# One short product at a time between products of 512 columns, and attention's later steps one step later

## What is computed

```python
x = x + einsum('bct,bcd->bdt', x, weights[itok])          # one 128x128 weight per batch
q, k, v = (proj(x, W) for W in (Wq, Wk, Wv))             # 1024 -> 1024, 16 heads of 64
q = q * minimum(cond, 4)
scores = where(causal, q @ k.T / 8, min)                  # 128 x 128 per head
x = x + (softmax(scores) @ v) @ Wo.T
```

## Time and profile before

| what | value |
|---|---|
| median of three runs | 1571.13 us |
| the profiled execution, span | 1569.4 us |
| TensorE busy | 1559.1 us (99%) |
| VectorE, ScalarE, GpSimd busy | 980.4, 818.9, 856.6 us |
| chain that ended last | TensorE 98%, DMA 1%, SyncE 1% |

### The profile page before, as it was taken

The page is one execution under the profiler, slowest core; times in us unless marked ns, Lnnn a source line. Parts: engine busy times, 40 slices in busy tenths (PEclk is TensorE's granted clock), DMA queues, the critical chain, the costliest instruction groups (busy, mean ns, idle before and its releaser), DMA issues.

```text
span 1569.4 us, 23424 instructions
## 1 busy us (share of the span) xinstructions
PE 1559.1 (99%) x7563; PEld 1311.9 (84%) x7563; DVE 980.4 (62%) x1748; ACT 818.9 (52%) x2221; POOL 856.6 (55%) x752
## 2 busy tenths in 40 slices
PE   9999999999999999999999999999999999999999
PEld 7888888888888888888888888888888878888887
DVE  6844454443367777777766777777777754555553
ACT  6645545543366666666666666666666522222220
POOL 1545645643255566557555566675577544555552
PEclk9999999999999999999999999999999999999999
DMA  9958888865856766667677466666675696444442
GB/s 329 334 212 275 307 285 297 301 214 215 308 182 197 206 207 199 210 188 199 186 240 238 152 172 212 186 182 201 182 195 159 222 367 238 168 161 167 163 163 85
DMA packets 192299, 341.46 MB, mean 218 GB/s; under 512 B 23986, under 2 KB 116402, under 8 KB 185010
## 3 DMA queue, kind: packets, MB, share of 16 engines
q1 hardware_dynamic: 191026, 331.59, 65.8%
q10 hardware_dynamic: 1152, 8.39, 1.4%
HBM read 184.70 MB, written 134.22 MB: 203 GB/s over the span
## 4 chain that ended last, share of the span: by engine, by line
PE 98%; DMA 1%; SPq 1%; POOL 0%; issue 0%; DVE 0%; ACT 0%; DVEq 0%
PE p_PJ L710 22%; PE p_PJ L711 22%; PE p_PJ L712 22%; PE p_SC L712 6%; PE p_SC L711 6%; PE p_SC L710 6%; PE p_PV L815 4%; PE p_LP L710 1%; PE p_PV L710 1%; PE p_PV L712 1%; PE p_PV L711 1%; PE p_LP L711 1%; PE p_LP L712 1%; PE p_PV L841 1%; PE p_LP L841 1%; DMA out<-t_xr 1%
## 5 line engine op out<-in xcount | busy, mean ns | idle before, releaser
L711 PE MATMUL p_PJ<-t_XL,t_WH 128*128 128x512 f32 x1008 | 394.1, 391 | 0.0
L710 PE MATMUL p_PJ<-t_XH,t_WH 128*128 128x512 f32 x1008 | 394.1, 391 | 0.0
L712 PE MATMUL p_PJ<-t_XH,t_WL 128*128 128x512 f32 x1008 | 392.1, 389 | 0.0
L1035 ACT ACTIVATE t_PP<-t_PP,t_st 128x128 f32<-128x128 f32 x512 | 199.5, 391 | 175.4 <-DVE t_st L1211 173.9
L1333 POOL TENSOR_TENSOR t_PP<-t_PP,t_st 128x512 f32<-128x512 f32 x128 | 133.4, 1042 | 205.7 <-DVE t_st L1215 205.7
L712 PEld LDWEIGHTS p_PJ<-t_XH,t_WL 128*128 128x128 f32 x1008 | 189.3, 188 | 40.4
L710 PEld LDWEIGHTS p_PJ<-t_XH,t_WH 128*128 128x128 f32 x1008 | 190.0, 188 | 33.8
L711 PEld LDWEIGHTS p_PJ<-t_XL,t_WH 128*128 128x128 f32 x1008 | 190.0, 188 | 32.3
L1229 DVE TENSOR_REDUCE t_AT<-p_PV 64x256 f32<-64x512 f32 x252 | 171.2, 679 | 23.7 <-ACT t_AC L1053 12.0
L1339 POOL TENSOR_TENSOR t_AT<-t_AT,t_AC 128x256 f32<-128x256 f32 x126 | 117.2, 930 | 125.5 <-DVE t_AT L1229 125.5
L1336 POOL TENSOR_TENSOR t_PS<-t_PT,t_PS 128x512 fp32r<-128x512 f32 x122 | 157.7, 1293 | 0.0
(11 more groups left out here) (254 smaller groups left out, 3545.8 us busy)
## 6 DMA issues: line engine op xcount, KB each, us to landing
t_XH<-xth_scratch SPq DMA_DIRECT2D x56, 512.0 KB, 6.5
t_XL<-xtl_scratch SPq DMA_DIRECT2D x56, 512.0 KB, 6.9
t_PT<-t_TB SPq DMA_DIRECT2D x580, 32.0 KB, 2.3
v_scratch<-t_VR SPq DMA_DIRECT2D x64, 256.0 KB, 4.5
xth_scratch<-t_XH SPq DMA_DIRECT2D x16, 1024.0 KB, 4.0
xtl_scratch<-t_XL SPq DMA_DIRECT2D x16, 1024.0 KB, 6.5
t_VX<-v_scratch SPq DMA_DIRECT2D x32, 512.0 KB, 5.7
at_scratch<-t_AT SPq DMA_DIRECT2D x126, 128.0 KB, 3.5
```

Source lines behind the costliest of these rows:

```text
L710: pe.matmul(bank, lh, rh, start=first, stop=False, skip_group_check=goes_on)
L711: pe.matmul(bank, lh, rl, start=False, stop=False, skip_group_check=goes_on)
L712: return pe.matmul(bank, ll, rh, start=False, stop=last, skip_group_check=goes_on)
L1035: act.activation(PP[:, u, h, :], PP[:, u, h, :], ACT.Exp, bias=st[:, 0, u, h:h + 1], scale=1.0, accum_out=st[:, 1, u, h:h + 1]).then_inc(a ...
```

## The change

Ticks become twelfths of a step, and each of the three matmuls of a 512-column product gets a third of a step of its own. Transposes, scores and values are put one by one a sixth of a step (`BETWEEN`) behind such a matmul: the four transposes from q + 5 1/6 on, the twelve score matmuls of a cell over four steps instead of two bursts, and the four value matmuls of a half over a step and a third. Where two kinds fall into the same gap, they stand side by side there. The anchor a moves from 21 to 22 steps, and with it all that hangs on it: scores, masks, exponentials, reciprocals, norms, turns, moves, halves, values and their sums, on all engines. `q_ev`, `kh_ev`, `kl_ev`, the splits at `quiet(cell)`, the loads and the output blocks keep their steps. The eight transposes of batch 0 stay a burst. One wait of the turn at cell 58 is joined by the usual one. The rest of the diff passes the new index m, h or k through.

```diff
-TICK = 4
+TICK = 12
+BETWEEN = 1 / 6
...
                 l0_a.put(q, (bb, h))
                 l0_x1.put(q + 0.75, (bb, h))
-                l0_b.put(q + 5, (bb, h))
+                for k in range(4):
+                    l0_b.put(q + 5 + BETWEEN + k / 3, (bb, h, k))
...
             for i in range(7):
                 for d in range(4):
-                    P_at.put(t + 4 * i + d, (p, i, d))
+                    for m in range(3):
+                        P_at.put(t + 4 * i + d + m / 3, (p, i, d, m))
...
                     for d in range(DC):
-                        step_at.put(t0 + 16 * c + 8 * i + d, (kind, n, d))
+                        for m in range(3):
+                            step_at.put(t0 + 16 * c + 8 * i + d + m / 3, (kind, n, d, m))
...
-                a = done + 5
+                a = done + 6
                 for u in range(GB):
                     k = u // 2
-                    sc_at.put(a + k, GB * n + u)
+                    for m in range(3):
+                        sc_at.put(a - 1 + u + BETWEEN + m / 3, (GB * n + u, m))
                     mask_at.put(a + 1 + 2 * k, GB * n + u)
...
-                    for z in range(2):
-                        pv_at.put(v, 2 * P + z)
+                    for i in range(4):
+                        pv_at.put(v + BETWEEN + i / 3, (2 * P + i // 2, i % 2))
...
-        def three(bank, lh, ll, rh, rl, first, last, goes_on=False):
-            pe.matmul(bank, lh, rh, start=first, stop=False, skip_group_check=goes_on)
-            pe.matmul(bank, lh, rl, start=False, stop=False, skip_group_check=goes_on)
+        def one(m, bank, lh, ll, rh, rl, first, last, goes_on=False):
+
+            if m == 0:
+                return pe.matmul(bank, lh, rh, start=first, stop=False, skip_group_check=goes_on)
+            if m == 1:
+                return pe.matmul(bank, lh, rl, start=False, stop=False, skip_group_check=goes_on)
             return pe.matmul(bank, ll, rh, start=False, stop=last, skip_group_check=goes_on)
 
+        def three(*operands):
+            one(0, *operands)
+            one(1, *operands)
+            return one(2, *operands)
...
-        def pe_values(U):
+        def pe_values(U, h):
             n, u, z = U // GB, U % GB, U % 2
             j, c = divmod(n, NC)
             P = U // 2
-            if z == 0:
+            if z == 0 and h == 0:
                 pe.wait_ge(pool_pt, P + 1)
...
-            elif n == 58:
-                dve.wait_ge(s_O, 32 * 32)
             elif k == 0:
                 dve.wait_ge(l_P, 160 * n)
+            if n == 58:
+                dve.wait_ge(s_O, 32 * 32)
```

More of the change, by code:

```diff
@@ L304, in cond_attention @@
             l0_x1.put(-4 + h, (0, h))
-            l0_b.put(-3 + h, (0, h))
+            for k in range(4):
+                l0_b.put(-3 + h, (0, h, k))
             l0_X.put(-2 + 0.75 * h, (0, h))
@@ L421, in cond_attention @@
         turns = [(b, half) for half in (1, 0) for b in range(GB)]
-        x1_load = At()
+        x1_load, out_step, out_add = At(), At(), At()
         for o in range(N_OUT):
+            for d in range(DC):
+                for m in range(3):
+                    out_step.put(T_END + 8 * o + d + m / 3, (o, d, m))
+            out_add.put(T_END + 8 * o + 7.75, o)
             x1_load.put(T_END + ((-4, -4, 8, 10)[o] if o < 4 else 8 * o - 20), o)
@@ L732, in pe_step @@
             n = 0 if kind == "q" else 1
-            if d == 0:
+            if d == 0 and m == 0:
                 pe_wait_bank(kind, item)
@@ L754, in pe_step @@
             z = x_at_(j)
-            mm = three(PJ[bank_of[kind, item]][:], lh, ll, x_chunk(XHP, z, d), x_chunk(XLP, z, d), d == 0, d == DC - 1)
-            if d == DC - 1 and kind == "q":
+            mm = one(m, PJ[bank_of[kind, item]][:], lh, ll, x_chunk(XHP, z, d), x_chunk(XLP, z, d), d == 0, d == DC - 1)
+            if d == DC - 1 and m == 2 and kind == "q":
                 mm.then_inc(pe_q, 1)
-            elif d == DC - 1:
+            elif d == DC - 1 and m == 2:
                 mm.then_inc(pe_k, 1)
@@ L812, in pe_values @@
                     pe.wait_ge(dve_M, 2 * P)
[L813 to L816, removed]
+            moving = PS[:, 2 * u + h].rearrange("p a q -> p (a q)")
+            mm = pe.matmul(PV2[:, z, 256 * h:256 * h + 256], VV[j % 2][:, u, 2 * c + h, :], moving, start=True, stop=True)
+            if h == 1:
+                mm.then_inc(pe_pv, 1)
         def pe_l0_a(bb, h):
@@ L832, in pe_l0_a, with pe_l0_b, pe_out_step @@
             three(bank[:], wh[:], wl[:], xh[h][:], xl[h][:], True, True).then_inc(pe_a, 1)
-        def pe_l0_b(bb, h):
+        def pe_l0_b(bb, h, k):
             bank = l0_bank(bb, h)
-            pe.wait_ge(act_x1, 2 * bb + h + 1)
-            if bb == 0 and h == 0:
+            if k == 0:
+                pe.wait_ge(act_x1, 2 * bb + h + 1)
+            if bb == 0 and h == 0 and k == 0:
                 pe.wait_ge(l_ident, 16)
[L839 to L847, removed]
+            tt = h * 4 + k
+            mm = pe.transpose(bank[:, k * 128:(k + 1) * 128], x_tile(bb)[:, tt * 128:(tt + 1) * 128], ident[:])
+            if k == 3:
+                mm.then_inc(pe_b, 1)
+        def pe_out_step(o, d, m):
             b, half = turns[o]
-            if d == 0:
+            if d == 0 and m == 0:
                 pe_wait_bank("o", o)
@@ L858, in pe_out_step @@
             rh, rl = wo_tile(quarter)
-            mm = three(PJ[bank_of["o", o]][:], XH[1][:, row, cols], XL[1][:, row, cols], rh[:, d % 4, :], rl[:, d % 4, :], d == 0, d == DC - 1)
-            if d == DC - 1:
+            mm = one(m, PJ[bank_of["o", o]][:], XH[1][:, row, cols], XL[1][:, row, cols], rh[:, d % 4, :], rl[:, d % 4, :], d == 0, d == DC - 1)
+            if d == DC - 1 and m == 2:
                 mm.then_inc(pe_o, 1)
@@ L1675, in sp_program @@
                     sp_load_x1(o)
-                if T_END * TICK <= tick < T_PAIR * TICK and tick % (DC * TICK) == DC * TICK - 1:
-                    o = (tick - T_END * TICK) // (DC * TICK)
+                for o in out_add(tick):
                     b, half = turns[o]
```

67 lines of the change are left out of this document (35 added, 32 removed).

## The result

The changed kernel takes 1649.3 us (median of 4 runs, 1648.71 to 1649.92) against 1571.03 us for the kernel before, measured beside it: ratio 1.0499, 95% interval 1.0484 to 1.0514. It is 78 us slower. The forecast was 42 us slower and a range that ended at 1630.

A forecast was written before the change was run, and what follows sets the result against it. TensorE's order was taken to set the time, with VectorE's own-row sum 0.73 us early. 1569.4 + 41.5 (chain) + 1.2 (transposes) - 0.3 (end of attention) = 1611.8 us; the runs' median, 1.7 over, 1613.5; range 1594 to 1630.

The forecast's parts named there:

- The chain of one cell: Attention, from one first value of half 0 to the next: 14.16 us with a split against TensorE's 13.33; 41.5 us in all.
- The split: VectorE's split of a weight piece, now ahead of half 1's own-row sum: 0.70 us in cells that have one.
- TensorE's part: First value of half 0 to end of half 1's last value: 17 large and 19 short matmuls, 6.11 us.
- the bound of +6: Attention's matmul pacing: large matmuls behind short ones dearer by 0.006 us, 0.1 a cell; zero taken, -5 to +6 kept.
- From the sum to TensorE: Handover from the end of VectorE's own-row sum to TensorE's next value: 0.05 us.
- Transposes: Pair stages: price of a transpose stays, each large matmul behind is disturbed, 62 groups x 4 x 0.005: +1.2 us.
- The end of attention: TensorE's last wait: two more large matmuls before it, -0.45 us, a queued VectorE sum about 0.2; together -0.3 us.
- a loss half as large: Rival, 8%: chain right but a link shorter than its rows, about 0.35 us a cell, 21 us: 1592.5 us.
- no change: Rival, 6%: the chain ends less than 0.73 us later and fits the margin before the value burst: 1572 us.
- faster: Rival, 6%: waits fit and short matmuls between large ones hide weight loads, 13.15 us a cell: 1560 us.
- The second wait on top: k's low part late at the first score, up to 0.2 us a cell or 12 us: 1626 us, inside the upper end.
- The upper end: Top of the forecast's own 1600 to 1628 us, made by +6 for pacing and the second wait.

The follow-up runs named there:

- shift alone: Kernel before with attention's anchor at 22 steps instead of 21, all bursts kept: 1607.58 us.
- q behind the exponentials: Changed kernel with q's high part one step later, behind the last exponential, and q's low part between the two turns: 1633.35 us.
- all splits moved: Changed kernel with q's high part behind the last exponential and the weight splits on VectorE, their stores and ScalarE's high halves 2.25 steps later: 1580.14 us.

## Why the prediction was wrong

- *What bounds the kernel, and what the margin is*: right. VectorE's own-row sum was 0.73 us early before and is the releaser now.
- *The chain of one cell*: its order was right in every link, and it closes on itself: each run that moves an item out of it shortens the cell, down to 13.35 with all of them out. Its length was 14.16 us with a split and measured 14.81; without a split 13.46 and 13.67. So the mechanism was right, and the step that failed is what three of its links cost, the split above all. Term by term, from the rows above:
  - *The split* is the step that failed most, a term that was sized too small: 0.70 was taken, 1.05 measured (714.93 to 715.98). In 48 cells 16.8 us. The row that I took the earlier trace rows was of a split that started ahead of GpSimd's next instruction. In its new place it starts behind one.
  - *TensorE's part*: 6.11 was taken, 6.30 measured (702.72 to 709.02). The first value behind a wait takes 0.19, not 0.118: 0.07 that had no term. And a large one with a short one between two large ones takes 0.35 (703.50 to 703.85), not 0.3455, some 0.12 in all: that I had kept as the bound of +6 and set to zero. In 61 cells 11.6 us.
  - *From the sum to TensorE*: 0.05 was taken, 0.15 measured (715.98 + 1.40 = 717.38 to 717.53). In 61 cells 6.1 us. The 0.05 had no row; before, nothing waited there.
  - The read, the exponentials, q's high part, reciprocal, norm and turn measured 0.81, 1.56, 0.47, 0.78 + 0.12, 0.26, 1.07 and 0.64, within 0.03 of their terms.
  - Together 34.5 us: 39.8 + 1.7 + 34.5 = 76.0, measured 74.0. The 2 us between them are in TensorE's part: it is 6.30 in the cells of 14.81 us, but 6.22 to 6.25 in those of 14.73 and of 13.67, where all later links agree within 0.04.
  - With the split alone put right the forecast would have been 1613.5 + 16.8 = 1630.3 us, at the end of the range; the other two terms are 17.7 us more.
- *Transposes*: +1.2 forecast, +1.7 measured alone (0.2 to 3.0 by the interval). The rival price (12.6 us back) is refuted.
- *The end of attention*: -0.3 forecast, +1.9 measured. The wait grew instead of shrinking by the two large ones that stand before it; I didn't test which link of it did.
- *The rivals*: a loss half as large, no change and faster are all refuted by the kernel after. (The 0.2268 of "faster" stands in no row that was shown; large matmuls in a row measure 0.2275.) The second wait on top is not in it; the run with the sum ahead of the split shows that it was near.
- *The upper end*: the two bounds that it names, 6 us for dearer matmuls and 12 for a second wait, give 1613.5 + 18 = 1631.5 us; 1628 was written. Apart from these no term of the chain could grow. It should have had the split beside GpSimd: a row of 1.24 us stood in the trace of before.

The missed price stands in the trace of before, on the other engine. GpSimd's sum of rows takes 0.73 us by itself and 1.24 when it starts behind VectorE's split at 713.51 (timeline of GpSimd in the kernel before, then in the kernel after):

```profile
713.56 1.24 POOL L1339 TENSOR_TENSOR t_AT<-t_AT,t_AC 128x256 f32<-128x256 f32 x1 [1.20 <-DVE t_AT L1229]
```
```profile
717.46 0.73 POOL L1360 TENSOR_TENSOR t_AT<-t_AT,t_AC 128x256 f32<-128x256 f32 x1 [1.95 <-DVE t_AT L1251]
```

Whichever starts second pays. The split ended some 0.55 us behind the end of GpSimd's instruction in each of four kernels: after (716.06 against 715.51), shift alone (715.75 against 715.20), q behind the exponentials (712.79 against 712.25), all splits moved (708.54 against 707.99). The Trainium skill, "SBUF — State Buffer", states under "Who interferes with whom" that a VectorE instruction with two inputs in SBUF contends with a GpSimd instruction that reads SBUF, and under "Summary: rules for kernel authors" that the second to issue blocks until the first is done. The four ends agree with it in the main: the split's length follows from where GpSimd's instruction ends (0.65 where it had ended, 1.13, 1.44), not from its own size. It is not exact: the split ends 0.55 us behind it, and its whole 0.65 after a full block would be 0.10 more. GpSimd's sum, likewise, ends 0.60 us behind the split (714.80 against 714.20), not 0.73. Which part of SBUF the two compete for, no run here shows. k's low part, with one input in PSUM, takes its 0.68 at 717.41 while GpSimd's sum at 717.46 takes its 0.73: neither is longer, which also agrees.

## What to carry to other kernels

When a step moves, its duration is a property of its new neighbours: look up which engine works beside the new place, and search the trace for the same pair in either order, since the cost may show on the other engine's rows. A loop whose end releases its own start turns each 0.1 us into 0.1 us per round, so every handover in it needs a row or a bound. Two halves of a change that are measured apart can close the loop through different links, so their losses need not add up. And an unhurried list of one engine (q's high part, the splits) can be put behind the critical steps, but then every engine of that side path has to move along: moving two of three left ScalarE waiting for a store.

## What the runs showed of the hardware

- A VectorE instruction with two SBUF inputs, 0.65 to 0.69 us by itself, takes up to 1.44 when it starts 0.4 us behind a GpSimd instruction of 1.29 us.
- Short matmuls cost the same one by one as in a burst, or a little more: a transpose with a large one 0.34 us against 0.11 + 0.2275, a cell of 68 matmuls 13.35 against 13.33 where nothing waits.
- The first matmul behind a wait holds up the next for 0.19 us instead of 0.118, and from the end of VectorE's sum to its start pass 0.15 us.
- With a last wait of 2.21 us TensorE ran the four values in 0.74 us; with 3.67 it ran them in 1.23, at half the clock (granted 1.00 and 0.50).
